# Value matmuls of two key tiles first, their sum matmuls after, in the pair blocks of an attention step

## The reference

```
qkv    = x @ w_qkv.T + b_qkv
scores = q @ k.T / sqrt(32)              # causal: later keys are masked out
attn   = softmax(scores)                 # exp(scores - max) / sum
out    = attn @ v
x = layernorm(x + out @ w_out.T + b_out)
hidden = relu((x @ sign(up_w).T) * up_scale)
x = layernorm(x + (hidden @ sign(down_w).T) * down_scale * output_scale)
```

## Time and profile before

| | |
|---|---|
| Median of 3 runs | 795.6 us (795.46 to 797.47) |
| Profiled execution, its own time | 801.23 us |
| Its span, first to last instruction | 799.5 us |
| PE busy | 746.0 us (93% of the span) |
| DVE busy | 456.0 us (57%) |
| ACT busy | 323.2 us (40%) |
| POOL busy | 345.9 us (43%) |
| Mean granted TensorE clock | 0.974 |

### The profile page before, as it was taken

How to read it: one execution, slowest core, us unless ns; L and a number is a source line. 1 busy time by engine, 2 the same in 40 slices (tenths; PEclk the granted TensorE clock), 3 DMA queues, 4 the chain that set the end, 5 groups by cost and what they waited for, 6 DMA issues and landing times.

```text
span 799.5 us, 11694 instructions
## 1 busy us (share of the span) xinstructions
PE 746.0 (93%) x4048; PEld 509.6 (64%) x4048; DVE 456.0 (57%) x1086; ACT 323.2 (40%) x631; POOL 345.9 (43%) x479
## 2 busy tenths in 40 slices
PE   6899899999999999999989897999999999999994
PEld 4687655655556455555554453588778877878882
DVE  3276386676766767758576662433277329433614
ACT  5111355555555655545555556532231223221220
POOL 4441456364553555544527534362244234323333
PEclk9999899999999999999997997999999999999998
DMA  6966263525545344344467440413002101000101
GB/s 233 311 166 184 68 178 114 146 81 144 156 112 157 95 134 145 92 145 124 130 188 219 145 162 5 155 43 119 14 14 105 27 14 39 14 1 2 52 1 52
DMA packets 44619, 85.71 MB, mean 107 GB/s; under 512 B 4880, under 2 KB 13584, under 8 KB 44432
## 3 DMA queue, kind: packets, MB, share of 16 engines
q1 hardware_dynamic: 35536, 79.72, 33.1%
q10 hardware_dynamic: 9024, 5.24, 2.3%
HBM read 55.33 MB, written 29.36 MB: 106 GB/s over the span
## 4 chain that ended last, share of the span: by engine, by line
PE 75%; DVE 15%; issue 4%; ACT 2%; DMA 2%; POOL 2%; ACTq 0%; SPq 0%; POOLq 0%; DVEq 0%
PE ps_heads L1013 9%; PE ps_unit L946 9%; PE ps_proj L906 8%; DVE heads_sb L805 7%; PE ps_proj L1056 7%; PE ps_score L983 6%; PE ps_score L1073 6%; PE ps_unit L1029 6%; PE ps_unit L1056 5%; PE ps_sum L1007 5%; PE ps_heads L1073 3%; PE ps_sum L1073 3%; DVE maxes L783 2%; PE ps_sum L991 2%; DVE heads_sb L807 2%
## 5 line engine op out<-in xcount | busy, mean ns | idle before, releaser
L681 ACT ACTIVATE probs<-ps_score 128x512 f32<-128x512 f32 (+3 forms) x360 | 170.8, 490 | 180.1 <-PE ps_score L983 171.3
L779 DVE CUSTOM_DVE_ANT_0 ps_unit<-ps_unit,causal 128x128 f32<-128x128 f32 (+3 forms) x256 | 121.9, 512 | 77.0 <-PE ps_unit L946 74.3
L625 POOL TENSOR_TENSOR hid_low<-hid_raw,hid_high 128x512 fp32r<-128x512 f32 x64 | 85.0, 1328 | 174.6 <-DVE hid_high L856 171.5
L946 PE MATMUL ps_unit<-stack 96*128 96x512 f32 (+3 forms) x384 | 134.4, 364 | 10.9 <-DVE maxes L783 4.3
L983 PE MATMUL ps_score<-stack 98*128 98x512 f32 (+2 forms) x360 | 134.9, 383 | 7.5 <-ACT probs L681 6.0
L594 POOL TENSOR_SCALAR_AFFINE_SELECT probs<-probs 128x128 f32<-128x128 f32 x256 | 73.9, 294 | 153.6 <-ACT probs L681 150.9
L946 PEld LDWEIGHTS ps_unit<-stack 96*128 96x128 f32 x384 | 72.6, 193 | 57.3 <-issue 17.4
L856 DVE CAST hid_high<-hid_raw 128x512 fp32r<-128x512 f32 x64 | 27.1, 424 | 131.1 <-ACT hid_raw L736 130.9
L783 DVE TENSOR_REDUCE maxes<-ps_unit 128x1 f32<-128x512 f32 x128 | 80.7, 684 | 26.0 <-PE ps_unit L946 25.6
L983 PEld LDWEIGHTS ps_score<-stack 98*128 98x128 f32 x360 | 69.3, 195 | 40.6 <-ACT probs L681 23.9
L1013 PE MATMUL ps_heads<-probs,v_rows 128*32 128x512 f32 (+3 forms) x768 | 84.5, 511 | 5.1 <-DVE heads_sb L807 3.3
(11 more groups left out here) (184 smaller groups left out, 1208.1 us busy)
## 6 DMA issues: line engine op xcount, KB each, us to landing
stack<-qk_parts SPq DMA_DIRECT2D x96, 256.0 KB, 4.7
qk_parts<-parts SPq DMA_DIRECT2D x32, 512.0 KB, 2.7
v_all<-h_even ACTq DMA_DIRECT2D x16, 256.0 KB, 3.4
v_rows<-v_all SPq DMA_DIRECT2D x8, 512.0 KB, 4.5
heads_t<-heads_sb SPq DMA_DIRECT2D x16, 256.0 KB, 2.6
raw<-up_w SPq DMA_DIRECT2D x8, 512.0 KB, 3.6
x_tile<-x_rows SPq DMA_DIRECT2D x16, 256.0 KB, 5.0
raw<-down_w SPq DMA_DIRECT2D x8, 512.0 KB, 3.8
```

Of the source, the lines that this page charges most:

```text
L625: nc.gpsimd.tensor_tensor(hid[1][:, (HM * s + n) % 3, :], hid_raw[:, n % 2, :], hid[0][:, (HM * s + n) % 3, :].bitcast(FP32), ALU.subtract ...
L681: nc.scalar.activation(probs[:, (NP * s + n) % RING, 0:width], score_bank(s, n)[:, off:off + width], ACT.Exp, scale=SCALE).then_inc(s_exp, 1)
L779: nc.vector.tensor_tensor_reduce(ps_unit[n % 3][:, 0:width], ps_unit[n % 3][:, 0:width], causal[:, HALF - width:], 1.0, NEG, ALU.add, ALU.max,
L946: nc.tensor.matmul(ps_unit[n % 3][:, 0:width], stack[s % 2][0:96, 1, f, h, i % 4 * P:(i % 4 + 1) * P], stack[s % 2][0:96, 0, c, h, 0:width ...
```

## The change

```
--- before.py
+++ after.py
@@ -142,7 +142,7 @@
         for g, at in enumerate(PAIRED if paired else ALONE[s % 2]):
             put(t + at, "pv", s, g)
             if g < FIRST_ADD or g >= LAST_ADD:
-                put(t + at, "sum", s, g)
+                put(t + at + (0.01 if paired else 0), "sum", s, g)
```

## The result

The changed kernel took 802.0 us in the median of 9 runs (797.28 to 804.36), the kernel before 795.94 us in the median of 9 (793.01 to 797.75). The ratio is 1.0059, with a 95% interval of 1.0032 to 1.0086, so it is slower beyond the 0.3% that a measurement can tell. A second measurement on one chip (12 runs against 35) gave 1.0042 (1.0015 to 1.0068). The forecast was 2.9 us, which is 1.0036. The two medians differ by 6.1 us, more than either ratio says, and 802.0 us lies above the stated range of 796.3 to 800.8, while 795.6 us times the ratio, 800.3 us, lies inside it: the runs of a kernel scatter over 5 to 7 us.

The account below looks back on a forecast made before the run. The prediction took PE as nearly full but waiting for DVE behind the block at slot 52. Six delays of 0.49 us gave 2.9 us on a median of 795.6, so 798.5 us, range 796.3 to 800.8.

Parts of the forecast that it names:

- The bound: Behind the block at slot 52, a later last sum delays DVE's reciprocal and, undiminished, PE's matmul at unit 3.
- The swaps at 13, 19.6 and 44: Reordering value and sum groups in these 18 blocks costs zero, within 0.02 us each or 0.4 us in all.
- Masks and ring slots: Inside the blocks, earlier second values and later release of probs slots cost zero; a late mask at most 0.29 us.
- The block at slot 52: With the score moved in, DVE starts 0.49 us later: about 0.16 the score, the rest an extra narrow-full-narrow change.
- The four terms of the sum: At slot 52, after the 128-column values start: 0.33 to score, 0.35 to sums, 0.46 between sums, 0.55 us to DVE.
- The wait for DVE: PE's wait at unit 3 grows about 0.3 us: 0.49 less 0.21 of PE's own delay.
- The third rival: Waits of 0.73 us grow to about 1.2 us and add a half-clock stretch of 4.9 us: 803.4 us; chance 0.07.
- Sum: Six blocks at slot 52 times 0.49 us give 2.9 us; the other 18 blocks add 0.0.
- The nearly free score: At slot 52 the width change overlaps weight loads or DVE's wait has slack: 0 to 1.7 us, 797.0 us; chance 0.30.
- Neither clock rival: A half-clock stretch of PE worth 4.9 us goes away (793.6 us, chance 0.05) or is added (803.4 us, chance 0.07).

Follow-up runs that it names:

- the short reciprocal: Last reciprocal of half 1 cut to one column in steps 0 to 5: changed kernel's step 51.62 to 50.83 us, the kernel before's 51.12 to 50.35 us.
- the swaps-only kernel: Against the kernel before: value, value, sum, sum in the sum blocks of steps 0 to 5, score still behind the sums; ratio 0.9981, step 51.11 us.
- the opposite move: Against the kernel before: block at slot 52, old order, moved ahead of one score (ratio 0.9978) or two (1.0262; 0.9967 with stack DMAs issued first).
- the one with steps of 54.5 us: Against the kernel before: block at slot 52, old order, moved two scores earlier, with its shift rows ahead of the stack DMAs; ratio 1.0262.
- the kernel with the score ahead: Against the kernel before: score piece put ahead of the whole block at slot 52, order value, sum, value, sum kept; ratio 1.0055, step 51.63 us.

## Why the prediction was right, point by point

- **The bound.** That the last sum's end reaches PE through DVE undiminished was right, and is shown by the short reciprocal: 0.79 us less on DVE is 0.79 us less in a step. The distance from reciprocal to unit 3 is 5.17 us with and without the change.
- **The swaps at 13, 19.6 and 44** at zero: right. The block at 44 kept its 3.14 us, and the swaps-only kernel its step of 51.11 us.
- **Masks and ring slots** at zero: right; the first value matmul of the second tile comes straight behind the first tile's, in one row of x16.
- **The block at slot 52** at 0.49 us: measured 0.50 us from the first value matmul to the reciprocal (2.16 less 1.66), and 0.51 us by the step. The four terms of the sum came out one by one: 0.79 us for the first two groups and the way to the score (0.46 + 0.33 forecast), 0.37 (0.35) and 1.00 (1.01). For its split, 0.16 us of the score itself and 0.33 us for the change of width, the runs give 0.17 us from the score's start to the next matmul's elsewhere, and 0.36 us beyond its own time for a projection in the score's place. The 0.36 was not measured with the score itself, and no run tells what in the change of width takes the time.
- **The wait for DVE** was to grow by about 0.3 us, the 0.49 less 0.21 of PE's own delay. This part was off. Where no wait for the DMAs disturbs it, it went from 0.73 to 0.90 us, 0.17 us more. PE itself was later than forecast: its projection matmul by 0.23 us (1.95 against 1.72 us from the first value matmul), but the first unit matmul by 0.34 us (4.93 to 5.27 us, first blocks of both traces). The two orders were compared at the projection's start, and that hid 0.1 us: the second start behind a narrow block also comes about 0.1 us later than elsewhere. Before, that fell ahead of the projections (0.28 us from the score to them, 0.17 us elsewhere); now it falls behind their start (0.56 us from the pair to the next score, 0.47 us before). It costs nothing, since DVE ends the wait either way. The third rival's "about 1.2 us" for this wait didn't fit the prediction's own growth of 0.3 us either; it was at most 0.90.
- **Sum**: 2.9 us forecast, 6 x 0.51 = 3.1 us by the steps. The first timing gave 4.7 us by its ratio (0.0059 x 795.94), with an interval of 2.5 to 6.9 us; the second 3.3 us. The agreement to 0.2 us is that of the steps; that the median of nine runs lay 3.5 us above the forecast of 798.5 stays open between the scatter and the clock. (The 804.2 us against the profiled execution should read 804.1.)
- **The rivals.** The nearly free score is excluded by the step. The stretches at half clock vary from run to run in both kernels, by more than the effect. Neither clock rival can be shown to be tied to the change, and inside the six steps neither happened: the granted clock stayed at 1.00 in all three traces that have the score in the block.

## What to carry to other kernels

When items of different kinds share one slot of a sorted plan, moving one of them by a hair lets anything with the same slot in between; read the order of the instructions, not the diff. Ahead of the matmul that another engine waits for, a matmul of another width cost its own time here and about twice as much again for the change of width, and the place to look for gains is the opposite move, as long as each queue's own order is kept. Where repeated steps can be read from the trace, their length tells half a microsecond that the time of the whole kernel can't.

## What the runs showed of the hardware

A full-width matmul of 512 columns among column-tiled ones cost 0.36 us beyond its own time, at a granted clock of 1.00 (steps of 51.70 and 51.34 us). The mean granted clock of a run lay between 0.971 and 0.987 for all kernels here but the one with steps of 54.5 us (0.962 to 0.972), and the time followed it: 794.1 us at 0.985 and 802.3 us at 0.974 for the same kernel before. That is more than twice the effect of the change. Behind waits of PE of 1.7 to 2.7 us the granted clock fell to 0.50 for 3.4 us each time in that slowest kernel; behind waits of up to 0.9 us it stayed at 1.00 in the changed kernel. In the kernel with the score ahead it fell once with no such wait in the 7 us before. The last landing signal of the three stack DMAs came 0.09 us ahead of the first unit matmul wherever PE had waited for it (248.45, 194.41 and 202.95 us in three traces).
